# First two attentions of a decoder kernel: scores in four 32-row groups, softmax one turn ahead, turns written out

## The reference, cut to what matters

```python
# A: causal self-attention
q, k, v = split(x @ W_in.T + b_in)            # 16 heads of 16
s = einsum('bnqd,bnkd->bnqk', q, k) * 0.25     # masked above the diagonal
x = layernorm(x + (softmax(s) @ v) @ W_out.T + b_out)
# B: cross-attention to a context
ref, sup = relu(x @ W_fc.T + b_fc), relu(ctx @ W_fc.T + b_fc)
q, k = ref @ W_q.T + b_q, sup @ W_k.T + b_k
s = einsum('bqhd,bkhd->bhqk', q, k) * 0.25
x = layernorm(x + ref + softmax(s) @ (sup @ W_v per head) + b_v)
```

## Time and profile before

| | |
|---|---|
| median of 3 runs | 1164.45 us (1162.76 to 1165.28) |
| the profiled execution's own time | 1164.86 us |
| its span, first to last instruction | 1163.0 us |
| mean granted TensorE clock | 0.949 |
| PE busy | 1030.0 us (89%) |
| DVE, ACT, POOL busy | 664.5, 403.6, 331.5 us |
| layers A and B, from the first matmul to the last logits | 12.9 to 246.0 us |

### The profile page before, as it was taken

The page is one execution under the profiler, slowest core; times in us unless marked ns, Lnnn a source line. Parts: engine busy times, 40 slices in busy tenths (PEclk is TensorE's granted clock), DMA queues, the critical chain, the costliest instruction groups (busy, mean ns, idle before and its releaser), DMA issues.

```text
span 1163.0 us, 18374 instructions
## 1 busy us (share of the span) xinstructions
PE 1030.0 (89%) x5995; PEld 799.9 (69%) x6004; DVE 664.5 (57%) x1043; ACT 403.6 (35%) x748; POOL 331.5 (29%) x556
## 2 busy tenths in 40 slices
PE   4898999858799999999999959967999997599995
PEld 3666766546688888888888834556777875388884
DVE  2777777743355555555555646744556562455555
ACT  1444444522222323322233222322455454133231
POOL 0122222251334344443434430110011002234341
PEclk9999999958899999999999988978999999699998
DMA  7000000006543333333333000001111101364421
GB/s 276 1 1 0 1 1 0 1 1 164 163 135 123 115 114 108 118 105 115 110 118 105 10 8 1 1 21 26 33 30 24 28 18 56 64 168 115 106 50 36
DMA packets 37378, 77.60 MB, mean 67 GB/s; under 512 B 6844, under 2 KB 17888, under 8 KB 36938
## 3 DMA queue, kind: packets, MB, share of 16 engines
q1 hardware_dynamic: 37046, 76.80, 22.6%
q0 software_dynamic: 288, 0.23, 0.2%
HBM read 69.83 MB, written 2.40 MB: 62 GB/s over the span
## 4 chain that ended last, share of the span: by engine, by line
PE 77%; DVE 7%; SPq 6%; ACT 3%; issue 3%; DMA 2%; POOL 1%; ACTq 0%; POOLq 0%; DVEq 0%
PE ps L932 28%; PE ps L943 14%; PE ps L503 5%; PE ps L445 4%; PE ps L613 3%; SPq L346 3%; PE ps L452 2%; SPq L398 2%; PE ps L822 2%; PE ps L514 2%; PE ps L528 2%; PE ps L706 1%; PE ps L757 1%; PE ps L801 1%; PE ps L797 1%
## 5 line engine op out<-in xcount | busy, mean ns | idle before, releaser
L932 PE MATMUL ps<-shared 128*128 128x512 f32 x1560 | 382.4, 395 | 6.0 <-POOL shared L1787 6.0
L932 PEld LDWEIGHTS ps<-shared 128*128 128x128 f32 x1560 | 298.0, 191 | 69.5 <-issue 6.4
L1255 ACT ACTIVATE shared<-pT 128x512 fp32r<-128x512 f32 x130 | 82.2, 632 | 307.6 <-DVE pT L1618 307.6
L1785 POOL CAST shared<-wraw 128x512 fp32r<-128x512 f32 (+1 forms) x130 | 91.6, 705 | 330.1 <-PE ps L943 293.0
L943 PE MATMUL ps<-shared 128*128 128x512 f32 x520 | 162.7, 394 | 11.6 <-DVE al L1621 11.5
L1614 DVE TENSOR_TENSOR e<-e,ps 128x512 f32<-128x512 f32 x130 | 89.3, 687 | 140.4 <-PE ps L932 134.0
L1621 DVE TENSOR_TENSOR al<-pT,shared 128x512 fp32r<-128x512 f32 x130 | 117.2, 902 | 90.8 <-ACT shared L1255 90.8
L1787 POOL TENSOR_TENSOR shared<-wraw,shared 128x512 fp32r<-128x512 f32 (+1 forms) x130 | 132.1, 1016 | 10.4
L1675 POOL TENSOR_SCALAR newton<-agg 128x1 f32<-128x1 f32 (+1 forms) x36 | 8.9, 249 | 416.2 <-DVE agg L1291 389.7
L943 PEld LDWEIGHTS ps<-shared 128*128 128x128 f32 x520 | 98.5, 190 | 34.0 <-DVE al L1621 13.2
L1618 DVE TENSOR_TENSOR pT<-e,kbd 128x512 f32<-128x512 f32 x130 | 100.4, 772 | 24.0 <-DMA kbd<-combine_C 9.6
(11 more groups left out here) (208 smaller groups left out, 1460.2 us busy)
## 6 DMA issues: line engine op xcount, KB each, us to landing
kbd<-combine_C SPq DMA_DIRECT2D x48, 512.0 KB
wraw<-in_C_w SPq DMA_DIRECT2D x48, 384.0 KB, 8.1
kbd<-combine_F SPq DMA_DIRECT2D x17, 512.0 KB
wraw<-in_F_w SPq DMA_DIRECT2D x17, 384.0 KB, 6.8
kbd<-kbd SPq DMA_DIRECT2D x96, 32.0 KB, 1.9
kT<-kbd SPq DMA_DIRECT2D x48, 32.0 KB, 1.8
c_x_t<-in_x_t SPq DMA_DIRECT2D x1, 1024.0 KB, 4.7
c_x_rows<-in_x_rows SPq DMA_DIRECT2D x1, 1024.0 KB, 7.0
```

The lines of the kernel that those rows point to most:

```text
L932: mm = pe.matmul(GU[t][s], w[u][:, (c * 2 + s) * P:(c * 2 + s + 1) * P], xx[:, c, t * HALF:(t + 1) * HALF], start=(i == 0), stop=(i == 5))
L1255: act.activation(ah[t][:, :], a2[t], ACT.Copy).then_inc(S("ah"), 1)
L1785: pool.tensor_copy(wh[u][:, lo:hi], wraw[k][:, lo:hi]).then_inc(S("m_wh"), 1)
```

## The change

All turns of A and B are written out as Python loops, without hardware loops. The pipeline has more stages: in turn t item t is projected, t-1 has its scores and softmax, t-2 its transposes and values, t-3 its output rows and division, t-4 its residual and layer norm, t-5 its x_T and t-6 the copy of it. Both halves of an item's scores lie in banks 0 to 3 at once, all projections go to PT, and ref and sup of B to OB.

The scores use the fact that 16 heads of 16 are 8 strips of 32 rows with two heads each. The keys are written only twice (k2: even heads, odd heads), by four ACT instructions of 128x128 instead of the two of DVE; scores of an item are 8 matmuls of depth 32 and 256 columns, in four row groups, each into its own bank. POOL makes no staged copies and keeps no rows: PE reads XT and CTXT, and DVE writes the normalized row into X directly. xb has two buffers. All 8 logits come after the last x_T. Masked biases bk2 are computed once for each layer (four small DVE instructions in all).

```diff
-            def scores(b, s, n):
...
-                for h in range(2):
-                    if L == "A":
-                        pe.matmul(sl[:, h, :], ident16[:, :], causal[:, :], start=True, stop=False)
-                    mm = pe.matmul(sl[:, h, :], qT[u][:, n, :], kbd[u][:, n, 4 * h:4 * h + 4, :],
-                                   start=(L == "B"), stop=True)
+            def context(i):
...
+                pe.wait_ge(S("ot"), i - 2)
+                pe_T(pe, OB[:, 0:D], W["B", "wfc"], XT[:, :, tok(b)])
+                pe_T(pe, OB[:, D:2 * D], W["B", "wfc"], CTXT[:, :, tok(b)]).then_inc(S("fcps"), 1)
+            def project(i):
+                if i > 1:
+                    pe.wait_ge(S("pc"), 4 * i - 4)
...
+            def scores(i):
+                pe.wait_ge(S("q"), 2 * i + 2)
+                pe.wait_ge(S("kb"), 4 * i + 4)
+                if i > 0:
+                    pe.wait_ge(S("sub"), 2 * i)
                 if L == "A":
+                    for r in range(4):
+                        pe.matmul(ps[:, r, :], ident16[:, :], causal[:, :], start=True, stop=False, skip_group_check=True)
+                for c in range(C):
+                    for r in range(4):
+                        lo = slice(32 * r, 32 * r + 32)
+                        mm = pe.matmul(ps[:, r, c * D:(c + 1) * D], qT[i % 2][lo, c, :], k2[i % 2][lo, c],
+                                       start=(L == "B"), stop=True, tile_position=(32 * r, 0), skip_group_check=True)
+                mm.then_inc(S("sps"), 1)
+            def transposes(i, u):
+                pe.wait_ge(S("exp"), 2 * i + u + 1)
+                if u == 0:
+                    pe.wait_ge(S("q"), 2 * min(i + 2, 2 * B))
+                    pe.wait_ge(S("kb"), 4 * min(i + 2, 2 * B))
+                    pe.wait_ge(S("v"), min(i + 2, 2 * B))
                 else:
+                    pe.wait_ge(S("pc"), 4 * i + 2)
...
+            for t in range(2 * B + 5):
+                (lp, _), (ls, _), (lv, _), (lo, _), (ly, _), (lx, _) = (item(t - n) for n in range(6))
+                if lv:
+                    transposes(t - 2, 0)
+                if ly == "A":
+                    out_project(t - 4)
+                if ly == "B":
+                    ref_rows(t - 4)
+                if lp == "B":
+                    context(t)
+                if lv:
+                    transposes(t - 2, 1)
+                if ls:
+                    scores(t - 1)
+                if lo:
+                    out_rows(t - 3)
+                if lp:
+                    project(t)
+                if lv:
+                    values(t - 2, 0)
+                    values(t - 2, 1)
+                if lx:
+                    x_T(t - 5)
+                if lo == "A":
+                    out_T(t - 3)
+            pe_logits(pe, "B", range(B))
...
+            def keys(i):                                    # ACT
+                for c in range(C):
+                    for n in range(2):
+                        act.activation(k2[i % 2][:, c, n, :], PT[0][:, D + c * P:D + (c + 1) * P], ACT.Identity,
+                                       bias=bk2[i // B][:, c, n:n + 1], scale=hmask[:, n:n + 1]).then_inc(S("kb"), 1)
...
+            for t in range(2 * B + 6):                      # ACT
+                (lp, _), (ls, _), (lv, _), (lo, _), (ly, _), _, (lx, bx) = (item(t - n) for n in range(7))
+                if ly == "A":
+                    out_T(t - 4)
+                if lx:
+                    act_x(act, lx, bx, MB[:, D:2 * D])
+                if lo:
+                    outputs(t - 3)
+                if lv:
+                    copies(t - 2, 0)
+                if lp == "B":
+                    context(t)
+                if lv:
+                    copies(t - 2, 1)
+                if lp:
+                    queries(t)
+                if ls:
+                    exps(t - 1, 0)
+                if lp:
+                    keys(t)
+                if ls:
+                    exps(t - 1, 1)
...
+            for t in range(2 * B + 4):                      # DVE
+                if ly:
+                    residual(t - 4)
+                if ls:
+                    unit(t - 1, 0)
+                if lo:
+                    normalize(t - 3)
+                if lp:
+                    values(t)
+                if ls:
+                    unit(t - 1, 1)
+                if ly:
+                    normalized(t - 4)
...
+            for t in range(2, 2 * B + 2):                   # POOL
+                if t - 1 < 2 * B:
+                    residual(t - 1)
+                L, b = item(t - 2)
+                pool_rstd(pool, L, b, t % 2)
```

More of the change, by code:

```diff
@@ L109, in build @@
         kbd = [sb(f"kbd{u}", [P, C, 8, P]) for u in range(2)]
+        k2 = [m[:, 0, 0:2 * C, :].rearrange("p (c s) k -> p c s k", c=C) for m in kbd]
+        bk2 = [sb(f"bk2{L}", [P, C, 2]) for L in "AB"]
         shared = [sb(f"shared{u}", [P, KV1 * G1 * P], F32R) for u in range(3)]
@@ L132, in build @@
         aT = sb("aT", [P, C, P])
-        xb = sb("xb", [P, D])
+        xb = [sb(f"xb{u}", [P, D]) for u in range(2)]
         z1 = sb("zsum", [P, D])
@@ L200, in build @@
         ps = ctx.enter_context(nc.psum_tensor("ps", [P, 8, HALF], F32))
-        SLOT = [ps[:, 2 * s:2 * s + 2, :] for s in range(2)]
+        SC = ps[:, 0:4, :].rearrange("p r (c s k) -> p r c s k", c=C, s=2)
         PT = [ps[:, 4 + s, :] for s in range(2)]
@@ L256, in before_done, with item @@
                 eng.wait_ge(S("xt"), nb(L, 1))
[L257 to L260, removed]
+                eng.wait_ge(S("xn"), nb(L, 0))
                 if p in NEXT_IS_MOE:
                     eng.wait_ge(S(f"{p}_cT"), 2 if p == "B" else 1)
[L264 to L286, removed]
+        def item(t):
+            return ("A", t) if 0 <= t < B else ("B", t - B) if B <= t < 2 * B else (None, None)
         def first(i):
@@ L507, in transposes @@
[L507 to L511, removed]
-                    for q in range(4):
[L513 to L530, removed]
@@ new lines, in transposes, with values @@
+                    for q in range(4):
+                        at_ = (h * 4 + q) * P
+                        mm = pe.transpose(PT[h][:, q * P:(q + 1) * P], e[u][:, at_:at_ + P], ident[:, :])
+                    mm.then_inc(S("tr"), 1)
+            def values(i, u):
+                pe.wait_ge(S("pc"), 4 * i + 2 * u + 2)
+                if u == 0:
+                    pe.wait_ge(S("v"), i + 1)
+                    if i > 0:
+                        pe.wait_ge(S("ot"), i)
+                    if i >= B - 2:
+                        pe.wait_ge(S("fc"), 4 * min(i + 3 - B, B))
+                for c in range(C):
+                    for m in range(4):
+                        head, j = 8 * c + 4 * u + m, (m // 2) * 4 + 2 * c + m % 2
+                        mm = pe.matmul(OB[32 * m:32 * m + 32, (2 * c + u) * P:(2 * c + u + 1) * P],
+                                       v[i % 2][:, head * VW:(head + 1) * VW], pT[u][:, j * P:(j + 1) * P],
+                                       start=True, stop=True, tile_position=(0, 32 * m))
@@ L541, in out_T @@
-            def out_T(c):
-                pe.wait_ge(S(f"{L}_an"), c + 1)
+                    mm = pe.transpose(MB[:, k * P:(k + 1) * P], oT[:, 0, k * P:(k + 1) * P], ident[:, :])
+                mm.then_inc(S("otr"), 1)
+            def out_T(i):
+                pe.wait_ge(S("an"), i + 1)
                 for k in range(C):
                     mm = pe.transpose(MB[:, k * P:(k + 1) * P], an[:, k * P:(k + 1) * P], ident[:, :])
[L545 to L549, removed]
@@ L561, in x_T @@
                 mm.then_inc(S("xtr"), 1)
-            return dict(L=L, project=project, project2=project2, scores=scores, transposes=transposes,
-                        values=values, out_rows=out_rows, out_T=out_T, out_project=out_project,
-                        ref_rows=ref_rows, x_T=x_T)
-        def pe_two(s, p, c, f):
-            (P_, pb), (C_, cb), (F_, fb) = (x or (None, None) for x in (p, c, f))
-            if f:
-                F_["out_rows"](fb, 0)
-            if c:
-                C_["scores"](cb, s, 1)
-            if f and F_["L"] == "B":
-                F_["ref_rows"](fb, s)
-            if f and F_["L"] == "A":
-                F_["out_T"](fb)
-            if p:
-                P_["project"](pb, s)
-            if f and F_["L"] == "A":
-                F_["out_project"](fb)
-            if p and P_["L"] == "A":
-                P_["project2"](pb, s)
-            if c:
-                C_["transposes"](cb, 0)
-            if p and P_["L"] == "B":
-                P_["project2"](pb, s)
-            if c:
-                C_["transposes"](cb, 1)
-                C_["values"](cb, s, 0)
-            if p:
-                P_["scores"](pb, 1 - s, 0)
-            if c:
-                C_["values"](cb, s, 1)
-            if f:
-                if not c:
-                    pe_logits(nc.tensor, F_["L"], range(EARLY))
```

(8 more changed lines are left out.)

370 lines of the change are left out of this document (150 added, 220 removed).

## The result

The changed kernel is slower: median 1188.84 us (1178.93 to 1195.63) against 1164.65 for the kernel before, ratio 1.0204 [1.0130, 1.0277], which is clear of 1 but not of 1.02. The forecast was 1144.5, its range 1138 to 1161. The profiled execution took 1188.79 us with a span of 1187.0. The kernel's executions differ with their mean granted clock, 1178.93 us at 0.927 and 1195.63 at 0.911, far more than the 0.2% that the forecast took for the noise.

What follows compares the result with a forecast made beforehand. PE was taken to bind layers A and B; afterwards a DVE, ACT, PE chain. Head 22, 15 distances 176.5 and drain 27.2 put the logits at 225.7 instead of 246.04, 20.3 us gained: 1144.5 us, range 1138 to 1161.

Steps and rivals of the forecast that it cites:

- the sum of the turns: Layers A and B: 15 distances from one item's scores to the next, 176.5 us in all.
- Values 0.33: DVE's write of the values, between division and second maximum in the chain of a turn: counted as 0.33 us.
- rival 4: Chain of a turn longer by handovers or a wait counted as hidden: 0.5 a turn, 8 us, 1152; chance 0.16.
- Rival 3: Clock falls in each turn as PE stands idle, doubling transposes and scores: 46 us more, 1190; chance 0.06.
- The four keys: ACT's four 128x128 key instructions an item, taken as 1.15 us from two queries at 0.61 together.
- the row groups: An item's scores on PE: sixteen 256-column records in four overlapping row groups, 0.86 us, seen within about 1.05.
- the row that they were taken from: Layer D's 16 numerator records of 64x128: 0.60 against 1.8 one after another, read as fourfold overlap.
- the head: Start of the stage up to the end of the first scores: 21.3 to 23.1 us, taken as 22.
- the busy times of DVE and ACT: Per turn, DVE 7.2 in A and 7.4 in B, ACT 7.2 and 7.9 us, all below PE.
- PE would no longer bind: With PE at 10 us of work, a chain through three engines sets the turn: 12.05 in A, 11.9 in B.
- The drain: From the last scores at 198.5 to the last logits at 225.7: 27.2 us, longer than before.
- what follows moves rigidly with the logits: Everything behind the last logits is untouched and waits for them, so only their end counts: 246.04 to 225.7.

Runs made afterwards that it cites:

- the last run: Third buffer for the values and early masks in A, against the changed kernel, without any useless matmul; 1153.83 us, ratio 0.9920 to the kernel before.
- half filling: Changed kernel with a third buffer for the values and 2, 4 and 1 useless matmuls in PE's gaps instead of 4, 8 and 3; 1149.91 us.
- full filling: Changed kernel, still two value buffers, with 4, 8 and in A 3 more useless bf16 matmuls in PE's gaps; 1164.48 us.
- the third buffer: Changed kernel with a third buffer for an item's values, so DVE's write waits on an item earlier; alone 1164.83 us.
- A's masks early and less filling: Against the third buffer with half the useless matmuls: A's masks behind the first transposes replace the 4 there, and A's 1 more goes; 1143.96 us.

## Why the prediction was wrong

Two steps failed, both in the sum of the turns (219.80 measured, 176.5 forecast); the rest was right within a few us.

1. "Values 0.33" in DVE's part of the chain. The instruction takes that long. But it waits until PE has multiplied with the buffer that it overwrites, and with two buffers that is values(t-2, 1), which stands behind project(t) in PE's list of the same turn. The forecast listed what PE's groups wait for and did not do it for this DVE instruction; rival 4 named two other waits and 0.5 a turn. Measured 1.22 in 13 turns. Taken away alone it gives 23.9 us.
2. Rival 3, the clock, was argued down with "none is as long" as 3.15. The idle pieces were found (1.4 twice a turn by the forecast, 0.8 to 1.0 and 1.9 to 2.3 in the trace), but that nothing shorter than the 3.15 of the one row lets the clock fall was inferred from that row alone. It fell behind pieces of 1.01 and 0.91 (the last run). In A and B it fell to 0.86 and 0.81 in two stretches of 80 us. The rival's 46 us was too much, because it doubled transposes and scores in every turn, while the scores came back to 1.15 to 1.35 and some turns kept the clock. Taken away alone it gives 20.2 us. That the rival's 1190 lies next to the measured 1188.84 is luck: its cause gives about half of the distance, the wait that nobody named gives the other half.

The two are not independent: alone 23.9 and 20.2, together (half filling) 219.80 - 183.27 = 36.5. The wait lengthened the idle pieces and so took the clock down too; at whole clock it is worth 13.17 - 12.05 = 1.1 a turn of B (full filling against half and the third buffer). What is left over 176.5 are 6.8 us of small terms, by the distances of the kernel with half the filling: 1.5 in the first and 0.5 each in the second and the last, 0.26 to 0.29 in a turn of A, 0.15 in one of B, 0.67 in the first turn with `context`, and 0.55 to 0.57 in the three behind it. In these four the output projection, about 0.9 on PE, stands ahead of `context` and was forgotten; that this is the cause is read from the order, no run changes it. The four keys take 1.50 and not 1.15 (L997), but they lie beside DVE's work, off the chain.

Right: the row groups (1.15 us, forecast 1.05 to 1.2, and 2.47 less than untiled), though the row that they were taken from shows less than it was read for: 1.8 against 0.60 is an overlap of three, not four; the head (first maximum at 21.15, forecast 22); the busy times of DVE and ACT; and that PE would no longer bind. The drain took 30.4 instead of 27.2 (240.95 to 271.37), 3.2 more. That what follows moves rigidly with the logits was wrong by a little, twice: from their end to the next transposes after takes 7.4 us where before takes 11.4, since DVE no longer runs beside POOL, and the rest of the kernel takes 2.6 more, for which no run gives the cause. The balance against before: logits 271.37 - 246.04 = 25.3 later, less 4.0, plus 2.6, gives 23.9, and the profiled executions differ by 1188.79 - 1164.86 = 23.9.

With both faults mended the kernel gives 1149.9, with A's masks early and less filling 1144.0: the forecast's time, but by another kernel.

Open: what exactly decides in a turn whether the clock falls (2.29 us of idle time stood ahead of half clock at 86.75 and of full clock at 148.61, and pieces of 1.0 in B cost the clock where pieces of 1.0 and 1.2 in A did not). And whether the useless matmuls in B could be replaced by useful work: it was not tried.

## What to carry to other kernels

When a change takes an engine off the critical path, the chain that takes over runs through its list in order: write down for every instruction of that chain, the short ones on the other engines too, which buffer it overwrites and who must have read it, and where that reader stands in its own list. A TensorE that becomes partly idle can lose its clock although no idle piece is longer than 1 to 2 us (here 1.01 and 0.91 a turn were enough), so the saved work comes back as slower work on the chain. Look at the granted clock of the stretch after such a change. Then first move real work of its own into the gaps (here the masks), and only then fill with useless matmuls, and no more than the gap holds.

## What the runs showed of the hardware

- The clock fell in the kernel after with idle pieces of 0.8 to 1.0 and 1.9 to 2.3 us a turn (0.78 in the turn of A shown, 0.86 and 0.81 in the long windows), and in the kernel without useless matmuls with 1.01 and 0.91 (0.89), where I had taken 3.15 for the shortest that matters. With six useless bf16 matmuls in a turn of B, about 1.4 us by 8 in 1.89 (an estimate), it stayed at 1.00.
- A DVE subtraction of 128x512 from two SBUF tiles took 0.77 us when POOL's 128x2048 of 4.5 was over and 3.97 to 4.19 beside it, in the kernel before as well. The eight `MAX8` just ahead of it, with one input, took 1.11 beside POOL's and 1.11 behind it:

```profile
246.43 4.62 POOL L1796 TENSOR_TENSOR shared<-c_x_t,shared 128x2048 fp32r<-128x2048 f32 x1
246.81 1.11 DVE L1582 MAX8 top<-pT 128x8 f32<-128x64 f32 x8
247.95 4.19 DVE L1584 TENSOR_TENSOR pT<-pT,top 128x512 f32<-128x512 f32 x1
```

- Sixteen 256-column f32 records of depth 32 in four row groups take 1.15 us, of full depth 3.62, a factor of 3.1. The Trainium skill, TensorE: Matmul & The Clock Gate, Measured speedup vs the span model, has 3.07 for four groups of 512 columns; the trace agrees.
- Four ACT instructions of 128x128 with a scale and a bias from a column take 1.51 together, a single one 0.47 (they overlap); with a bias alone two take 0.62 and a single one 0.36 (the kernel after, means of 50 to 240 us).
